# A two-layer graph kernel: three subtractions go to GpSimd, x's second half is loaded sooner, the bias split comes later

## The chip, the core and the metric

The kernel runs on one core of a Trainium2 chip. The metric is the device time of one execution in microseconds (us). The core has five engines, each with its own instruction queue: TensorE (PE, matrix products, with its weight load PEld), VectorE (DVE), ScalarE (ACT), GpSimd (POOL) and SyncE (SP, which here only starts transfers). They order their work by semaphores alone.

## What is computed

Two message-passing layers over a graph of 3125 nodes with 53125 edges. A message is a linear function of the target's row, the source's row and one number of the edge; messages are added up at their target, and self loops are added.

```python
def _mp_layer(x, src, dst, edge_attr, W, b):
    loops = jnp.arange(n); src2 = cat(src, loops); dst2 = cat(dst, loops)
    ea2 = cat(edge_attr, zeros)
    msg = jnp.concatenate([x[dst2], x[src2], ea2], axis=1) @ W + b
    return jax.nn.relu(jax.ops.segment_sum(msg, dst2, num_segments=n))
h = relu(_mp_layer(x, ..., W1, b1))          # 64 -> 128 columns
out = log_softmax(_mp_layer(h, ..., W2, b2)) # 128 -> 64 columns
result = layernorm(x + out)
```

## The kernel before

The sum over edges is made as a product with the adjacency matrix. That matrix (3125 x 3125, bf16) is built on the chip: edges are sorted by target, so every 5 targets own a window of at most 128 edges; there are 625 windows, handled in 79 sets of 8.

**Start.** DVE and PE find where each window's edges begin (`pick_row`, `offset`, the last step of `offset` raises `off_ready`, one count for each of 5 blocks j of 125 windows). GpSimd fetches each block's edges with an indirect transfer (`gather_edges(j)`, L400, into `pairs`, counted by `pairs_in[j]`) and the edges' numbers with another (`gather_attrs(j)`, L404). DVE turns block 0 into keys (L535 to L547), PE transposes them, ACT copies them to `keys` (`copy_keys`, L880, L882).

**The loop over sets.** For set k, DVE makes the one-hot matrices (`onehots(k)`, L569: one instruction over 8 windows, from set 12 on over 7, the eighth being made by GpSimd's `last_onehot(k)`, L441). PE multiplies them (`build(k)`, L1057, 8 products into one of two PSUM buffers) and ACT copies the result into the adjacency matrix (`evacuate(k)`, L909). `onehots(k)` waits until `build(k-3)` is done, since there are three one-hot buffers; `build(k)` waits for `evacuate(k-2)`. PE runs `build` 4 sets ahead of layer 1: in round b it builds set b + 4 and multiplies the 8 adjacency blocks of set b with x (`layer1`, L1079). Layer 1 of target group 0 waits for `evacuate(3)`. After its 12th product PE builds set 6 and only then goes on to the x of groups 12 to 24.

**x in three pieces.** x is float32, the products are bf16, so x is split into a high, a middle and a low piece in `x3`. ACT copies the high piece (`cast_x`, L864), a subtraction leaves a rest in `x_rest` (`rest_of_x`, L581), ACT copies the middle piece (`cast_middle_x`, L868), and another subtraction makes the low one (`low_of_x`, L586). This is done for groups 0 to 11 (i = 0, XA = 12) and 12 to 24 (i = 1). Layer 1 needs middle and low of the half it reads (`xm_ready`, `xl_ready`).

**Bias in three pieces.** The bias rows are split in the same way: `cast_bias(k)` (ACT, L860), `bias_rest(k)` (DVE, L593). When all three pieces are there (`bp_ready` 3), SP sends them with nine small transfers to `bw` (L1253); they are first used by `hidden(0)` near 56 us.

**Edge numbers.** DVE sums them (`attr_sums`, L556, one instruction a set, sets 16 to 20 for block 0). SP writes the sums to DRAM (L1258) and reads them back in another layout (L1261); GpSimd splits them (`split_sums(0)`, before its one-hot of set 24). SP's queue has the nine bias transfers ahead of L1258.

**SP's queue** at the start: targets (L1229), x's first half (L1231), three weight transfers, six bias transfers, a wait for `pairs_in[0]`, x's second half (L1244), two more bias rows.

All queues are written out by hand in this order; no planner reorders them.

Of the kernel before, what the change touches and what calls it, by code (L numbers as in the profile page):

```python
# [100 lines left out]
def gnn(nc, x, x_tiles, dst, edges, edge_attr, W1, b1, W2, b2, out, E):  # L101
# [3 lines left out]
    with ExitStack() as ctx:  # L105
# [260 lines left out]
        def _(gp):  # L366
# [31 lines left out]
            def gather_edges(j):  # L398
                gp.wait_ge(off_ready, j + 1)
                gp.indirect_dma_start(pairs[:, j, 0:2 * (SLOTS - LOOPS)], None, edges,  # L400
                                      bass.IndirectOffsetOnAxis(off_idx[:, j:j + 1], 0)).then_inc(pairs_in[j], 16)

            def gather_attrs(j):
                gp.indirect_dma_start(attrs[:, j, 0:SLOTS - LOOPS], None, edge_attr,  # L404
                                      bass.IndirectOffsetOnAxis(off_idx[:, j:j + 1], 0)).then_inc(attrs_in[j], 16)

            gather_edges(0)
            gather_attrs(0)
            gather_edges(1)
            gather_attrs(1)  # L410
            for j in range(2, J):
                gather_edges(j)
            for j in range(2, J):
                gather_attrs(j)
# [68 lines left out]
        def _(dve):  # L483
# [98 lines left out]

            def low_of_x(i, a, b):

                dve.wait_ge(xm_ready, i + 1)
                dve.tensor_tensor(x3[:, a:b, 2 * XC:2 * XC + C], x_rest[:, a:b, :], x3[:, a:b, XC:XC + C], ALU.subtract)\  # L586
                   .then_inc(xl_ready, 1)

            def bias_rest(k):

                before = brows[VHALF:128, :] if k == 0 else brest[VHALF:128, k - 1, :]
                dve.wait_ge(bp_ready, k + 1)
                dve.tensor_tensor(brest[VHALF:128, k, :], before, bpart[VHALF:128, k, :], ALU.subtract).then_inc(br_ready, 1)  # L593
# [41 lines left out]
            rest_of_x(0, 0, XA)  # L635
            bias_rest(0)
            dve.wait_ge(consts, 7)
# [6 lines left out]
            onehots(3)  # L644
            low_of_x(0, 0, XA)
            onehots(4)
            rest_of_x(1, XA, G)

            for k in range(5, NSETS):
# [3 lines left out]
                onehots(k)  # L653
                if k == 6:
                    low_of_x(1, XA, G)
                if k == 9:
                    bias_rest(1)
# [184 lines left out]
        def _(act):  # L842
# [26 lines left out]

            cast_bias(0)  # L870
            cast_x(0, 0, XA)
# [66 lines left out]
            def cast_middle(i):  # L938
                a, b = EPILOGUES[i]
                act.wait_ge(rest_ready, i + 1)  # L940
                act.activation(z3[:, a:b, C:2 * C], u[i % 2][:, 0:b - a, 0:C], ACT.Copy).then_inc(mid_ready, 1)

            evacuate(0)
            evacuate(1)
            cast_x(1, XA, G)
            for k in range(2, LEAD):
                evacuate(k)
            for b in range(NSETS):
                if b + LEAD < NSETS:
                    evacuate(b + LEAD)  # L950
                if b == 0:
                    cast_middle_x(1, XA, G)
                if b == 2:
                    cast_bias(1)
                if b == 6:
                    cast_bias(2)
# [271 lines left out]
        def _(sp):  # L1228
            sp.dma_start(dst_rows, dst).then_inc(dst_in, 16)  # L1229
            sp.wait_ge(dst_in, 16)  # L1230
            sp.dma_start(x_nat[:, 0:XA, :], x_tiles[:, 0:XA, :]).then_inc(xnat_in[0], 16)  # L1231
            sp.dma_start(w1c[:, :], W1[0:2 * C, :]).then_inc(w_in, 16)
            sp.dma_start(w2c[:, 0:C], W2[HID:2 * HID, :]).then_inc(w_in, 16)
# [5 lines left out]
            for m in range(1, EP):  # L1239
                at_m = VFROM + m * KB  # L1240
                sp.dma_start(brows[at_m:at_m + 3, :], row_b1.broadcast_to([3, HID])).then_inc(b_in, 16)
                sp.dma_start(brows[at_m + 3:at_m + KB, :], row_w1.broadcast_to([KB - 3, HID])).then_inc(b_in, 16)
            sp.wait_ge(pairs_in[0], 16)
            sp.dma_start(x_nat[:, XA:G, :], x_tiles[:, XA:G, :]).then_inc(xnat_in[1], 16)  # L1244
            sp.dma_start(b2w2[:, 0, :], b2.rearrange("(a n) -> a n", a=1).broadcast_to([Q, C])).then_inc(b2_in, 16)
# [69 lines left out]
```

## Time and profile before

| what | us |
|---|---|
| median of 3 runs | 195.45 (195.19 to 196.38) |
| the profiled execution, its time | 196.11 |
| the profiled execution, its span | 194.0 |
| PE busy in it | 173.6 |
| DVE busy in it | 161.8 |
| ACT busy in it | 114.5 |
| POOL busy in it | 99.2 |

The span runs from the first to the last instruction of one profiled execution. A row of a timeline gives the start, the duration, the engine, the line and the tiles written and read; what stands in square brackets is the idle time ahead of it and what ended that. Instructions overlap slightly at their ends, so the distance between starts is the real cost of one in a row of them. The chain of work that ended last is followed back from the last instruction.

### The profile page before, as it was taken

The page shows a single profiled execution, that of the slowest core. Times are in us where ns is not written, and L with a number is a line of the kernel's source. Part 1 is how long each engine was busy: PE and PEld are TensorE (multiplying, and loading weights), DVE is VectorE, ACT ScalarE, POOL GpSimd, SP SyncE. Part 2 cuts the span into 40 slices and gives each one's busy share as a digit, 9 for nine tenths or more (in the row PEclk, how much of TensorE's full clock was granted, in tenths as well). Part 3 has the DMA queues.
Part 4 walks back from the last instruction along what each step waited for, and adds up shares of the span by engine and source line. Part 5 has one row for each costly group of instructions (what it writes and reads, how often), then busy time and mean ns, then how long its engine had stood idle before and what let it go on. Part 6 is the DMA issues. An engine that isn't in the chain of part 4 may idle for free.

```text
span 194.0 us, 5193 instructions
## 1 busy us (share of the span) xinstructions
PE 173.6 (89%) x2050; PEld 157.6 (81%) x2051; DVE 161.8 (83%) x407; ACT 114.5 (59%) x197; POOL 99.2 (51%) x192
## 2 busy tenths in 40 slices
PE   7677577999699999989999999999999999999940
PEld 2124476998699898979999999999999999999940
DVE  0889999999997999999888979737619969889773
ACT  2425897888698989878989989972311102022201
POOL 6388504797697989699999969700000000000000
PEclk9969999999999999999999999999999999999996
DMA  1336200000000000000000000000000010100010
GB/s 44 103 89 155 57 3 2 6 1 4 1 6 1 4 1 4 2 1 4 0 3 0 5 3 0 0 3 5 0 0 5 8 35 0 42 9 22 20 25 20
DMA packets 9032, 3.35 MB, mean 17 GB/s; under 512 B 8240, under 2 KB 8557, under 8 KB 9007
## 3 DMA queue, kind: packets, MB, share of 16 engines
q1 hardware_dynamic: 8207, 2.08, 5.1%
q0 software_dynamic: 800, 0.93, 2.2%
q8 instruction: 17, 0.28, 0.6%
q14 instruction: 8, 0.07, 0.1%
HBM read 2.18 MB, written 0.81 MB: 15 GB/s over the span
## 4 chain that ended last, share of the span: by engine, by line
PE 59%; DVE 26%; DMA 7%; issue 3%; POOL 2%; ACT 0%; DVEq 0%; POOLq 0%
PE pset L1126 18%; DVE oh L569 15%; PE acc L1079 15%; PE acc L1126 9%; PE pset L1057 8%; DMA se<-se_scratch 3%; DMA adj<-in_edges,adj 3%; PE acc L1027 2%; PE epb L1120 2%; PE epb L1109 2%; DVE adj L556 2%; DMA se_scratch<-adj 2%; POOL oh L441 1%; PE epb L1097 1%; DVE adj L581 1%
## 5 line engine op out<-in xcount | busy, mean ns | idle before, releaser
L909 ACT ACTIVATE adj<-pset 125x1000 bf16<-125x1000 f32 (+1 forms) x79 | 78.5, 996 | 11.7 <-PE pset L1057 8.8
L441 POOL TENSOR_SCALAR oh<-iota,keys 128x125 bf16<-128x125 bf16 x132 | 78.3, 618 | 11.8 <-PE pset L1057 11.3
L569 DVE TENSOR_TENSOR oh<-iota_bank,keys 128x1764 bf16<-128x1764 bf16 (+4 forms) x81 | 83.1, 1052 | 0.5 <-PE pset L1057 0.4
L1079 PE MATMUL acc<-x,adj 125*125 125x195 bf16 x625 | 65.3, 248 | 0.3 <-DVE x L586 0.3
L1057 PE MATMUL pset<-oh 128*128 128x125 bf16 x625 | 48.2, 218 | 8.5 <-DVE oh L569 4.5
L1079 PEld LDWEIGHTS acc<-x,adj 125*125 125x125 bf16 x625 | 54.7, 137 | 0.9 <-issue 0.5
L1057 PEld LDWEIGHTS pset<-oh 128*128 128x128 bf16 x625 | 38.9, 97 | 12.7 <-ACT adj L909 6.0
L1126 PE MATMUL pset<-z,adj 125*125 125x192 bf16 x425 | 36.8, 246 | 0.0
L1126 PEld LDWEIGHTS pset<-z,adj 125*125 125x125 bf16 x425 | 35.5, 136 | 0.1
L988 ACT ACTIVATE x<-x 125x192 f32<-125x192 f32 (+2 forms) x6 | 2.6, 427 | 32.4 <-DVE x L737 32.4
L1126 PE MATMUL acc<-z,adj 125*125 125x192 bf16 x200 | 17.5, 246 | 0.0
L1126 PEld LDWEIGHTS acc<-z,adj 125*125 125x125 bf16 x200 | 16.8, 136 | 0.0
L601 DVE TENSOR_REDUCE u<-acc 125x65 f32<-125x195 f32 x25 | 8.9, 355 | 8.6 <-PE acc L1079 8.3
L1027 PE MATMUL acc<-adj 128*128 128x512 bf16 x31 | 11.3, 526 | 1.2 <-DVE adj L492 1.2
L1027 PEld LDWEIGHTS acc<-adj 128*128 128x128 bf16 x32 | 4.0, 127 | 6.5 <-issue 4.4
L400 POOL DMA_INDIRECT adj<-in_edges,adj x5 | 6.3, 1270 | 4.7 <-DVE adj L519 3.5
L728 DVE TENSOR_REDUCE x<-pset 125x64 f32<-125x192 f32 x17 | 5.4, 351 | 3.5 <-PE pset L1126 3.5
L556 DVE SCALAR_TENSOR_TENSOR adj<-adj 125x128 bf16<-125x128 f32 x25 | 7.4, 297 | 0.0
L404 POOL DMA_INDIRECT adj<-in_edge_attr,adj x5 | 6.0, 1208 | 1.5 <-issue 1.5
L1109 PE MATMUL epb<-turn,w1c 128*128 128x375 f32 x16 | 6.8, 504 | 0.0
L1120 PE MATMUL epb<-w2c,turn 128*125 128x128 f32 x48 | 6.8, 277 | 0.0
L622 DVE TENSOR_TENSOR u<-epb,z 125x192 f32<-125x192 f32 (+1 forms) x9 | 3.0, 337 | 4.1 <-ACT z L936 4.1
(125 smaller groups left out, 151.2 us busy)
## 6 DMA issues: line engine op xcount, KB each, us to landing
x_nat<-in_x_tiles SPq DMA_DIRECT2D x1, 406.2 KB
x_nat<-in_x_tiles SPq DMA_DIRECT2D x1, 375.0 KB
out<-x SPq DMA_DIRECT2D x2, 187.5 KB
out<-x SPq DMA_DIRECT2D x3, 93.8 KB
adj<-in_dst SPq DMA_DIRECT2D x1, 208.5 KB
bw<-adj SPq DMA_DIRECT2D x9, 1.0 KB
out<-x SPq DMA_DIRECT2D x1, 125.0 KB
adj<-in_edges,adj POOLq DMA_INDIRECT x5, 5.1
```

What stands on the lines that cost most here:

```text
L400: gp.indirect_dma_start(pairs[:, j, 0:2 * (SLOTS - LOOPS)], None, edges, bass.IndirectOffsetOnAxis(off_idx[:, j:j + 1], 0)).then_inc(pairs ...
L441: ins = gp.tensor_scalar(oh[k % 3][:, OWN, side, 0:Q], iota1[:, 0:Q], keys[:, place(k * SET + OWN), side, 0:1], None, ALU.is_equal)
L556: dve.scalar_tensor_tensor(out=se_junk[:, j * WD + r, :], in0=d_f[:, j, :], scalar=float(r), in1=attrs[:, j, :], op0=ALU.is_equal, op1=ALU ...
L569: ins = dve.tensor_tensor(out=oh[k % 3][:, at_w:at_w + m, :, 0:2 * PAIRS].rearrange("p w t (q e) -> p (w t) q e", e=2), in0=iota_p.unsquee ...
L601: dve.tensor_reduce(u[i % 2][:, m, C:2 * C + 1], acc[g % 2][0:Q, 0:XW].rearrange("p (t c) -> p c t", t=3), AX.X, ALU.add)\
L909: ins = act.activation(bands[c][0:Q, :, at_w:at_w + n * WD].rearrange("p h (w e) -> p h w e", e=WD), rows[:, 0:n, 0:WD * G].rearrange("p w ...
L1027: pe.matmul(acc[1][:, :], still[:, 0:128], still, start=True, stop=True)
L1057: ins = pe.matmul(pset[k % 2][:, i // 4, i % 4 * 128:i % 4 * 128 + WD * G], oh[k % 3][:, i, 0, :], oh[k % 3][:, i, 1, 0:Q], start=True, st ...
L1079: ins = pe.matmul(acc[g % 2][0:Q, 0:XW], block_of_adj(g, h), x3[:, h, 0:XW], start=(h == 0), stop=(h == G - 1))
L1109: pe.matmul(epb[:, 0, 0:n], w1c[:, :], flat(i)[:, 0:n], start=True, stop=False)
L1120: ins = pe.matmul(z_cols(b - a)[:, m, :], flat(i)[:, m * Q:(m + 1) * Q], w2c[:, :], start=True, stop=True)
L1126: ins = pe.matmul(bank2(g)[0:Q, :], block_of_adj(g, h), z3[:, h, :], start=(h == 0), stop=(h == G - 1))
```

## The change

Three of the four subtractions of x move from DVE to GpSimd: `low_of_x(0)`, `rest_of_x(1)` and `low_of_x(1)`; `rest_of_x(0)` stays on DVE. On GpSimd they stand behind the fourth gather of edges, with the fifth between the second and third of them, and four gathers of edge numbers come behind all that. ACT's `cast_x(1)` moves ahead of `evacuate(0)`, and `cast_middle_x(1)` from behind `evacuate(4)` to behind `evacuate(1)`. SP issues x's second half right behind the first, after a wait for the fourth offset in place of the first block's edges; weights and biases follow. The bias split moves back: `cast_bias(0)` from before `cast_x(0)` to round 2, `cast_bias(1)` from round 2 to 6, `cast_bias(2)` from 6 to 10, `bias_rest(0)` from before set 0 to behind set 8, `bias_rest(1)` from behind set 9 to behind set 12.

```diff
@@ gpsimd
+            def rest_of_x(i, a, b):
+                gp.wait_ge(xs_ready, i + 1)
+                gp.tensor_tensor(x_rest[:, a:b, :], x_nat[:, a:b, :], x3[:, a:b, 0:C], ALU.subtract).then_inc(xs_rest, 1)
+            def low_of_x(i, a, b):
+                gp.wait_ge(xm_ready, i + 1)
+                gp.tensor_tensor(x3[:, a:b, 2 * XC:2 * XC + C], x_rest[:, a:b, :], x3[:, a:b, XC:XC + C], ALU.subtract)\
+                  .then_inc(xl_ready, 1)
             gather_edges(0)
+            gather_edges(1)
             gather_attrs(0)
-            gather_edges(1)
-            gather_attrs(1)
-            for j in range(2, J):
-                gather_edges(j)
-            for j in range(2, J):
+            gather_edges(2)
+            gather_edges(3)
+            low_of_x(0, 0, XA)
+            rest_of_x(1, XA, G)
+            gather_edges(4)
+            low_of_x(1, XA, G)
+            for j in range(1, J):
                 gather_attrs(j)
@@ vector
             rest_of_x(0, 0, XA)
-            bias_rest(0)
...
             onehots(3)
-            low_of_x(0, 0, XA)
             onehots(4)
-            rest_of_x(1, XA, G)
...
                 onehots(k)
-                if k == 6:
-                    low_of_x(1, XA, G)
-                if k == 9:
+                if k == 8:
+                    bias_rest(0)
+                if k == 12:
                     bias_rest(1)
@@ scalar
-            cast_bias(0)
             cast_x(0, 0, XA)
...
+            cast_x(1, XA, G)
             evacuate(0)
             evacuate(1)
-            cast_x(1, XA, G)
+            cast_middle_x(1, XA, G)
...
-                if b == 0:
-                    cast_middle_x(1, XA, G)
                 if b == 2:
+                    cast_bias(0)
+                if b == 6:
                     cast_bias(1)
-                if b == 6:
+                if b == 10:
                     cast_bias(2)
@@ sync
             sp.dma_start(x_nat[:, 0:XA, :], x_tiles[:, 0:XA, :]).then_inc(xnat_in[0], 16)
+            sp.wait_ge(off_ready, 4)
+            sp.dma_start(x_nat[:, XA:G, :], x_tiles[:, XA:G, :]).then_inc(xnat_in[1], 16)
             sp.dma_start(w1c[:, :], W1[0:2 * C, :]).then_inc(w_in, 16)
...
-            sp.wait_ge(pairs_in[0], 16)
-            sp.dma_start(x_nat[:, XA:G, :], x_tiles[:, XA:G, :]).then_inc(xnat_in[1], 16)
```

## Rows read from the trace of the kernel before

**Rows 1.** Busy time of each engine in three stretches, with the granted clock (PEclk).
```profile
20.00:25.00 5.00, 2.55 (x34) 1.94 (x32) 5.00 (x6) 4.29 (x6) 2.41 (x2) 1.00 0.19 48
...
40.00:50.00 10.00, 9.10 (x122) 8.16 (x120) 9.93 (x23) 8.02 (x10) 7.27 (x14) 1.00 0.05 2
...
100.00:150.00 50.00, 50.00 (x632) 48.60 (x629) 35.83 (x66) 31.72 (x56) 23.27 (x40) 1.00 0.01 2
```

**Rows 2.** The chain that ended last, 7 to 47 us: start, us, what.
```profile
7.58 5.02 DMA adj<-in_edges,adj
...
16.06 4.55 DVE oh L569 x4
20.61 0.86 DVE x L586
...
22.59 0.93 DVE adj L581
...
25.76 0.93 DVE x L586
...
45.26 1.51 DMA se_scratch<-adj
```

**Rows 3.** Timeline of DVE, 11 to 45 us.
```profile
11.05 0.16 DVE L519 SCALAR_TENSOR_TENSOR adj<-adj 125x1 int32<-125x1 f16 x1
...
12.62 0.29 DVE L535 TENSOR_SCALAR adj<-adj,thr_neg 125x128 f32<-125x128 int32 x1 [0.64 <-DMA adj<-in_edges,adj]
...
15.40 0.36 DVE L593 TENSOR_TENSOR adj<-adj 64x128 f32<-64x128 f32 x1
15.80 0.23 DVE L638 COPY iota_bank<-iota 128x63 f32<-128x63 f32 x1
...
44.95 0.28 DVE L556 SCALAR_TENSOR_TENSOR adj<-adj 125x128 bf16<-125x128 f32 x1
```

**Rows 4.** The five edge gathers (L400): issue ns min/median/max, then time to landing.
```profile
L400 POOL DMA_INDIRECT adj<-in_edges,adj x5: 1212/1212/1501, 7.6 to 17.0; - x5
...
DMA to landing us min/median/max: 4.2/5.1/6.5
```

**Rows 5.** DMA queue of SP: packets, MB and share, 9.4 to 12.5 us.
```profile
q1 hardware_dynamic: 214, 0.08, 9.5%
```

**Rows 6.** The same queue, 12.6 to 18 us.
```profile
q1 hardware_dynamic: 182, 0.43, 23.1%
```

**Rows 7.** Timeline of SP's issues: x's second half, then the nine bias transfers.
```profile
12.61 0.26 SPq L1244 DMA_DIRECT2D x_nat<-in_x_tiles  x1
...
34.27 5.64 SPq L1253 DMA_DIRECT2D bw<-adj  x9
```

**Rows 8.** POOL's groups by line and shape: busy us, mean ns of one.
```profile
L441 POOL TENSOR_SCALAR oh<-iota,keys 128x125 bf16<-128x125 bf16 x132 | 78.3, 618 | 11.8 <-PE pset L1057 11.3 <-ACT keys L882 0.5
...
L425 POOL TENSOR_TENSOR se_rest<-se,stats 125x5 f32<-125x5 f32 x5 | 1.1, 218 | 0.4
...
L382 POOL CAST ident<-ident 128x125 bf16<-128x125 f32 x1 | 0.3, 291 | 0.1
```

**Rows 9.** Timeline of ACT, 15 to 28 us.
```profile
15.56 0.86 ACT L868 ACTIVATE x<-adj 125x768 bf16<-125x768 f32 x1
...
19.99 0.89 ACT L864 ACTIVATE x<-x_nat 125x832 bf16<-125x832 f32 x1
20.78 1.89 ACT L909 ACTIVATE adj<-pset 125x1000 bf16<-125x1000 f32 x2
...
27.57 0.31 ACT L860 ACTIVATE adj<-adj 64x128 bf16<-64x128 f32 x1
```

**Rows 10.** Timeline of PE, 22 to 24 us.
```profile
22.74 0.60 PE L1057 MATMUL pset<-oh 128*128 128x125 bf16 x8 [1.38 <-ACT adj L909]
23.18 0.84 PE L1079 MATMUL acc<-x,adj 125*125 125x195 bf16 x8
```

**Rows 11.** Timeline of POOL, the first one-hot that it makes.
```profile
30.89 1.20 POOL L441 TENSOR_SCALAR oh<-iota,keys 128x125 bf16<-128x125 bf16 x2 [8.18 <-PE pset L1057]
```

More of the change, by code:

```diff
@@ L581, in rest_of_x @@
                 dve.tensor_tensor(x_rest[:, a:b, :], x_nat[:, a:b, :], x3[:, a:b, 0:C], ALU.subtract).then_inc(xs_rest, 1)
[L583 to L587, printed above, removed]
             def bias_rest(k):
```

## The prediction, as put on record

> **What bounds the kernel now.** I read the busy time by stretch first, then the chain that ended last, then the timelines of the engines at the start. From 100 to 150 us PE is busy for all 50 us; from 40 to 50 DVE is busy 9.93 of 10 and PE 9.10; from 20 to 25 DVE is busy 5.00 of 5 and PE only 2.55 [rows 1]. So PE sets the end, but what it can start on is handed to it late by DVE. The chain goes through DVE's one-hots, and between them through three of DVE's subtractions for x, 0.86, 0.93 and 0.93 us of it; at 45.26 it passes to the DRAM write of block 0's edge sums [rows 2]. That write follows the last of DVE's attribute sums, at 44.95 [rows 3], and GpSimd and PE wait for its return. Before 12.6 us the chain is the first gather of edges, 5.02 us from 7.58 [rows 2], for which DVE idles 0.64 us [rows 3]. So the whole kernel hangs on how early DVE reaches its work of 45.26. Everything behind that point waits on other instructions of the chain and on nothing with a clock of its own, so a lead there is a lead at the end. I count the lead there.
>
> **First gather: lead 0.5.** Today three weight and six bias transfers run beside it: SP's queue moved 0.08 MB in 214 packets from 9.4 to 12.5 us [rows 5]. After the change these come later, and x's second half is issued only at the fourth offset's end, 11.05 + 0.16 = 11.21 [rows 3]. The five gathers land 4.2 to 6.5 us after their issue begins; the first has the longest issue, 1.50 us against 1.21 [rows 4]. With the best transfer it would land at 7.58 + 4.2 + 0.29 = 12.07. DVE is free at 12.62 - 0.64 = 11.98, so the gain lies between 0 and 0.62. I take 0.5, since the neighbours that the best gather lacked are what is taken away here.
>
> **Before the first one-hot: lead 0.3, less 0.07.** `bias_rest(0)` goes from in front of the iota copy, 15.80 - 15.40 = 0.40 us [rows 3]; it comes back behind set 8. But the one-hots also wait for ACT's copy of the keys, which comes from PE's transposes and moves with the gather alone; from the chain's order, with the first one-hot at 16.06 [rows 2] and the copy done near 15.67 (the middle cast follows it at 15.56 with a small overlap, [rows 9]), 0.33 of it can be used and I lose 0.02 to 0.1 to the wait. The first one-hot starts at 16.06 - 0.5 - 0.3 = 15.25. As the bias subtraction returns later, this is no lead at 45.26; the loss of 0.07 is.
>
> **Three subtractions off DVE: lead 2.72.** 0.86 + 0.93 + 0.93 [rows 2]. This is the gain if DVE never waits in their place.
>
> **What they cost on GpSimd.** The trace has no wide subtraction there. GpSimd's subtraction of 5 columns takes 0.218 us and its cast of 125 columns 0.291 [rows 8]: (0.291 - 0.21)/120 = 0.7 ns a column over a fixed 0.21 or so, which for 768 and 832 columns is 0.73 and 0.77 us. The compare of 125 columns takes 0.618 [rows 8], so 3.4 ns a column: 2.8 and 3.0. I take the middle, 1.8 and 1.9: two operands are read for each column where the cast reads one, while the compare does more per column than a subtraction.
>
> The Trainium skill (GPSIMD Engine Reference, "Performance versus the Vector engine") gives 4497 ns for a float32 `tensor_tensor` of 2048 columns. By that my estimate would be 1.69 and 1.83 us, the middle cast would come some 0.2 us sooner than below and the sum would be 2.5 in place of 2.3; no row of this trace has such an instruction, so it stays beside the sum.
>
> **Does anything wait for them?** I walk through the new order.
> - x's second half is issued at 11.25. Today it is issued at 12.61 [rows 7], and by 18.0 its queue had moved 0.43 [rows 6] of the 0.47 MB of x and the two bias rows behind it: about 5.4 us. It lands at 16.65. ACT's `cast_x(1)`, 0.89 us [rows 9], ends at 17.5. The first `evacuate` started at 18.05 today and would be due at about 17.0, so it is held 0.5; nobody needs it before `build(2)`.
> - `cast_middle_x(0)`, 15.56 + 0.86 today [rows 9], ends at 15.92. GpSimd's fifth edge gather, its seventh transfer, starts at 17.0 today, and each takes 1.21 and a gap of 0.3 [rows 4]; in the new order the fifth transfer is the fourth gather of edges and ends near 15.15. So `low_of_x(0)` runs 16.0 to 17.8 and `rest_of_x(1)` 17.8 to 19.7.
> - ACT ends `evacuate(1)` at 19.4, waits until 19.7, casts until 20.6 and then evacuates at 0.95 each (1.89 for two, [rows 9]): set 2 until 21.55, set 3 until 22.5.
> - PE: `build(4)` at 21.6 (22.74 today). The first eight products of layer 1 at 22.55 (23.18 today [rows 10]), `build(5)` until 23.8, four products, `build(6)` until 24.6. `low_of_x(1)`, after the fifth gather, ends at 23.15 and is hidden by 1.4 us.
> - ACT, always busy now: sets 4, 5, 6 until 25.75, `cast_bias(0)`, 0.31 [rows 9], until 26.05. DVE has nine one-hots of 1.115 (4.55 for four in a row with overlap, [rows 2], less 0.09) and comes to `bias_rest(0)` at 15.25 + 10.03 = 25.28. So **DVE waits 0.8 us there**: the queue of one-hots stands behind a bias subtraction that nobody needs soon. This is the new stall.
> - After that DVE is the slowest again. PE and ACT get 0.3 further ahead, as `bias_rest(1)` moves behind set 12.
> - The nine bias transfers occupy SP for 5.64 us, from 34.27 today [rows 7]. `cast_bias(2)` in round 10 comes at about 37.0, so SP is free at 42.65, and the sums' write is due at 45.26 - 2.35 = 42.9. Hidden with 0.25 us to spare; I charge 0.05.
> - The four gathers of edge numbers now end at 23.15 + 6.1 = 29.3. GpSimd's first one-hot began at 30.89 [rows 11] and is needed by `build(12)`, by my walk near 32.7. Hidden.
> - ACT's earlier bias casts, gone from the start, held nothing: `cast_x(0)` behind it was done before DVE needed it.
>
> **Sum.** 0.5 + 2.72 - 0.07 - 0.8 - 0.05 = 2.3 us. The profiled execution's span goes from 194.0 to 191.7 and its time from 196.11 to 193.8; against the median of 195.45, which lies 0.66 under it, the forecast is 193.2 us, 1.2% less.
>
> **Rivals.**
> - *A, the forecast*: gain 1.4 to 3.1. The upper end is a GpSimd as fast as its cast (middle cast right behind `evacuate(1)`, 0.3 us sooner, and the bias wait shrinks) with the wait of 0.8 nearly gone: 0.6 + 2.72 - 0.2. The lower end is no lead from the gather and a bias wait of 1.2. Chance 0.6.
> - *B, GpSimd at the compare's price*: 2.8 and 3.0 us. The pair in front of `cast_middle_x(1)` takes 2.1 us longer, ACT waits with all its evacuations behind the cast, layer 1 begins 2.1 later and DVE waits 2.9 at `bias_rest(0)` and before it for free one-hot buffers. Gain 0.2: 195.2 us. For it: it is the only arithmetic of GpSimd with many instances in the trace. Against: a compare with a scalar of each partition is another form. Chance 0.2.
> - *C, the load or SP's queue eats it*: x's second half lands 1 us later because four gathers cross it, and the same chain through ACT moves by 0.9; or the nine bias transfers end behind the sums. Gain 1.0: 194.4. Chance 0.12.
> - *D, slower*: GpSimd takes the compare's 0.618 us for 125 columns in full proportion, 4.9 ns a column, that is 3.8 and 4.1. The pair takes 4.2 us longer than I assume, `low_of_x(1)` then ends behind `build(6)` by a further 0.8, and DVE loses more than the 2.72 it saved: 2.3 - 4.2 - 0.8 = 2.7 us lost, 198.1. It decides from a pair price of about 6 us (no gain) and 8 us (1% slower). PE would also idle 3 us in a row; today's granted clock stays 1.00 with PE busy 2.55 of 5 [rows 1], which leaves open what a longer gap does. Chance 0.08.
>
> **How the numbers follow.** The likeliest is A, 193.2 us. The range reaches from A's best, 192.3, over C and B, to 195.6, leaving out D and a little at each end. A measurement of this kernel tells about 1% (1.95 us) from no change. A's gain lies above that in three quarters of its cases, the rest with B and C is within 1%: faster 0.47, same 0.45, slower 0.08.
>
> **What would show it.** In the changed trace: DVE starts L535 near 12.1; the first one-hot near 15.25; GpSimd's subtractions take 1.8 to 1.9 us each; ACT's middle cast of x's second half starts near 19.7; layer 1 starts near 22.5; DVE idles about 0.8 us ahead of `bias_rest(0)`, released by ACT; SP's write of the first edge sums is issued near 42.9 and not behind the bias transfers; from there every row stands 2.3 us earlier. I am wrong if a subtraction takes over 2.5 us, if the first gather still lands at 12.6, or if SP's write waits for SP itself.

## The result, and the profile after

Over 14 executions each the changed kernel took 194.53 us in the middle (193.82 to 196.10), the kernel before 195.76 (195.17 to 196.38). The ratio is 0.995, with a 95% interval of 0.993 to 0.9971: faster by 0.5%, or 1.0 us (the two middles are 1.2 us apart), where 1.2% had been forecast. A second group of 12 executions gave the same ratio, 0.995 (0.9925 to 0.9975). The time lies inside the range given. Two executions at a much lower clock throughout (298.94 us of the kernel before, 199.47 us of an edited kernel) are left out of every ratio and middle.

The profiled execution of the changed kernel does not show that: its span is 192.0 us against 194.0, with a time of 194.07 against 196.11, a gain of 2.0. Its start goes almost as the prediction walked it. (The changed kernel has line numbers of its own: its one-hots are L583, its bias transfers L1258, its write of the sums L1263.) DVE's timeline, with the lines that answer to [rows 3]:

```profile
11.93 0.29 DVE L549 TENSOR_SCALAR adj<-adj,thr_neg 125x128 f32<-125x128 int32 x1
12.13 0.56 DVE L550 TENSOR_SCALAR adj<-adj 125x128 f32<-125x128 int32 x1
...
15.09 10.12 DVE L583 TENSOR_TENSOR oh<-iota_bank,keys 128x2016 bf16<-128x2016 bf16 x9 [0.27 <-ACT keys L886]
25.96 0.29 DVE L601 TENSOR_TENSOR adj<-adj 64x128 f32<-64x128 f32 x1 [0.75 <-ACT adj L865]
...
42.61 0.28 DVE L570 SCALAR_TENSOR_TENSOR adj<-adj 125x128 bf16<-125x128 f32 x1
```

The keys begin at 11.93 without any wait (forecast 12.1), nine one-hots run without a break, and then DVE waits 0.75 us for ScalarE's bias cast (forecast 0.8). POOL's timeline:

```profile
11.45 1.21 POOL L404 DMA_INDIRECT adj<-in_edge_attr,adj  x1 [0.30 <-issue]
...
15.82 1.54 POOL L415 TENSOR_TENSOR x<-adj,x 125x768 bf16<-125x768 f32 x1
17.80 1.76 POOL L410 TENSOR_TENSOR adj<-x_nat,x 125x832 f32<-125x832 f32 x1 [0.44 <-ACT x L869]
...
20.99 1.67 POOL L415 TENSOR_TENSOR x<-adj,x 125x832 bf16<-125x832 f32 x1
```

The three subtractions take 1.54, 1.76 and 1.67 us. ACT's timeline, which answers to [rows 9]:

```profile
16.83 0.90 ACT L869 ACTIVATE x<-x_nat 125x832 bf16<-125x832 f32 x1 [1.09 <-DMA x_nat<-in_x_tiles]
17.63 1.88 ACT L913 ACTIVATE adj<-pset 125x1000 bf16<-125x1000 f32 x2
19.60 0.91 ACT L873 ACTIVATE x<-adj 125x832 bf16<-125x832 f32 x1
20.41 2.77 ACT L913 ACTIVATE adj<-pset 125x1000 bf16<-125x1000 f32 x3
```

ACT now stands still for x's second half, in front of the first evacuation; before, it asked for it at 19.99 and had no wait [rows 9]. PE's timeline ([rows 10]):

```profile
21.44 0.61 PE L1062 MATMUL pset<-oh 128*128 128x125 bf16 x8 [1.05 <-ACT adj L913]
22.33 0.89 PE L1084 MATMUL acc<-x,adj 125*125 125x195 bf16 x8 [0.28 <-ACT adj L913]
```

And SP's issues ([rows 7]):

```profile
37.25 5.64 SPq L1258 DMA_DIRECT2D bw<-adj  x9
42.94 0.46 SPq L1263 DMA_DIRECT2D se_scratch<-adj  x1
44.80 0.27 SPq L1266 DMA_DIRECT2D se<-se_scratch  x1
```

The write of the edge sums is issued at 42.94, 2.3 us sooner than the 45.26 of [rows 2], and right behind the ninth bias transfer. The chain shows that it takes longer from there:

```profile
42.94 1.85 DMA se_scratch<-adj
44.80 2.92 DMA se<-se_scratch
```

1.85 us where it was 1.51 [rows 2]. So of the lead of 2.3 us 2.0 are left, down to the end.

The same chain shows what the start now hangs on:

```profile
11.19 5.61 DMA x_nat<-in_x_tiles
...
16.83 0.91 ACT x L869
...
17.80 1.77 POOL adj L410
...
19.60 0.91 ACT x L873
20.51 1.78 ACT adj L913 x2
...
25.62 0.32 ACT adj L865
...
25.96 0.29 DVE adj L601
```

It no longer passes through the first gather, the first keys or DVE's first one-hots. It goes from the fourth offset over the landing of x's second half to ACT, and comes back to DVE only at the bias subtraction, for which DVE had been waiting.

The two profiled executions are 2.04 us apart (196.11 and 194.07), the middles only 1.23. The one of before lies 0.35 over the middle of its 14, the one of the changed kernel 0.46 under that of its own: 2.04 - 0.35 - 0.46 = 1.23. What is to be explained is why that pair of traces is not the typical pair.

### The profile page after: what moved, and what is told of

It is laid out like the page before. It is cut to its first block, busy times and chain, and to the rows that moved or that the text cites. A ratio compares the mean times of both kernels' runs of the same rounds, so it can differ in the third digit from the quotient of the medians.

```text
span 192.0 us, 5193 instructions
## 1 busy us (share of the span) xinstructions
PE 173.6 (90%) x2050; PEld 157.6 (82%) x2051; DVE 159.1 (83%) x404; ACT 113.7 (59%) x197; POOL 104.3 (54%) x195
## 4 chain that ended last, share of the span: by engine, by line
PE 60%; DVE 19%; DMA 8%; issue 4%; POOL 3%; ACT 3%; DVEq 0%; POOLq 0%
PE pset L1131 18%; PE acc L1084 15%; DVE oh L583 10%; PE pset L1062 9%; PE acc L1131 9%; DMA se<-se_scratch 3%; DMA x_nat<-in_x_tiles 3%; PE acc L1032 2%; PE epb L1125 2%; PE epb L1114 2%; DVE adj L570 2%; ACT adj L913 2%; DMA se_scratch<-adj 2%; POOL oh L455 1%; DVE adj L531 1%
## 5 line engine op out<-in xcount | busy, mean ns | idle before, releaser
L583 DVE TENSOR_TENSOR oh<-iota_bank,keys 128x1764 bf16<-128x1764 bf16 (+4 forms) x81 | 83.0, 1053 | 0.8 <-PE pset L1062 0.4
L913 ACT ACTIVATE adj<-pset 125x1000 bf16<-125x1000 f32 (+1 forms) x79 | 77.7, 994 | 9.6 <-PE pset L1062 7.4
L1131 PE MATMUL acc<-z,adj 125*125 125x192 bf16 x200 | 17.5, 246 | 0.0
L1131 PEld LDWEIGHTS acc<-z,adj 125*125 125x125 bf16 x200 | 16.8, 137 | 0.0
L400 POOL DMA_INDIRECT adj<-in_edges,adj x5 | 6.4, 1285 | 5.1 <-DVE adj L533 4.4
L939 ACT ACTIVATE base<-epb 125x192 f32<-125x192 f32 (+1 forms) x9 | 2.9, 318 | 6.1 <-PE epb L1125 6.1
```

The lines of the kernel that those rows point to most:

```text
L583: ins = dve.tensor_tensor(out=oh[k % 3][:, at_w:at_w + m, :, 0:2 * PAIRS].rearrange("p w t (q e) -> p (w t) q e", e=2), in0=iota_p.unsquee ...
L913: ins = act.activation(bands[c][0:Q, :, at_w:at_w + n * WD].rearrange("p h (w e) -> p h w e", e=WD), rows[:, 0:n, 0:WD * G].rearrange("p w ...
L1131: ins = pe.matmul(bank2(g)[0:Q, :], block_of_adj(g, h), z3[:, h, :], start=(h == 0), stop=(h == G - 1))
```

## The experiments

All of them are edits of the changed kernel unless said otherwise. Ratios are to the kernel before, run in the same group; for the changed kernel itself the ratio is 0.995 in both groups in which it ran. It did not run in the groups of `before_again`, `fill`, `bias_mix` and `dve_subs`, nor in that of `port_free`, `cold`, `combo` and `port_combo` (on another chip than the second group); these are compared with it through the ratios.

### The changed kernel again

> The changed kernel once more, nothing edited: what the other kernels of this group are compared with, and a second trace of it. Theory 1 (the walk was right, the forecast was read off an execution of the kernel before that lay 0.35 us over its own median): the lead at SP's write of the first edge sums is 2.3 us again and the middle of the runs is 1.2 to 2.0 us under the kernel before. Theory 2 (a part of the executions of the changed kernel has one more delay of about 1.5 us, which the profiled one did not have): the runs fall again in two groups, near 194.2 and near 195.8.

Ratio 0.995 (0.9925 to 0.9975). Both theories have a part. Sorted by mean granted clock, its 12 executions fall in two groups: eight with a clock over 0.975 took 193.42 to 194.18, four at 0.975 or less took 194.97 to 195.46. With the first 14 executions: 18 of 26 are over 0.975 and 8 at or under it. The middles of the groups differ by 1.3 us (193.96 and 195.31) and 1.5 us (194.33 and 195.80). For the kernel before in the same group they differ by 0.4 (15 executions with 195.29, 8 with 195.69). The bound of 0.975 was set after the times were known, and it is a rough mark: one execution of 195.20 had a clock of 0.994. The lead at the write of the sums was not 2.3 again: it is issued at 43.36, where the first changed trace has 42.94, as x's second half, on which the chain runs here too, came later (ACT's cast at 17.33 instead of 16.83) and DVE's wait grew to 1.05 us. First ACT's timeline of this trace, then DVE's:

```profile
17.33 0.90 ACT L869 ACTIVATE x<-x_nat 125x832 bf16<-125x832 f32 x1 [1.42 <-DMA x_nat<-in_x_tiles]
```

```profile
26.47 0.29 DVE L601 TENSOR_TENSOR adj<-adj 64x128 f32<-64x128 f32 x1 [1.05 <-ACT adj L865]
```

Its chain at the write:

```profile
43.36 1.81 DMA se_scratch<-adj
```

### The kernel before again

> The kernel before, nothing edited, for a second trace of it. The profiled execution of before had a span of 194.0 us, while half of its 23 executions of the first group lie under 193.4. If the execution on which the prediction rests was a late one, this trace shows where: the same order of work with a span nearer 193.3, and some 0.6 us less at one place, most likely in a transfer (the first gather, or the edge sums' way through DRAM), and the lead of the changed kernel over it is then under 2 us from there on. If the span is again 194.0, that reason falls.

One execution of 195.61 us, span 193.6. The trace on which the prediction rests was a late one: the write of the sums is issued at 44.66 here and at 45.26 there. The place is at the start, DVE's instructions for the first keys. This trace first, then the rows next to [rows 3] in the earlier one:

```profile
12.45 0.29 DVE L535 TENSOR_SCALAR adj<-adj,thr_neg 125x128 f32<-125x128 int32 x1 [0.41 <-DMA adj<-in_edges,adj]
...
12.90 0.23 DVE L540 TENSOR_SCALAR adj<-adj 125x128 f32<-125x128 f32 x1
...
15.47 4.55 DVE L569 TENSOR_TENSOR oh<-iota_bank,keys 128x2016 bf16<-128x2016 bf16 x4
```

```profile
13.08 0.57 DVE L540 TENSOR_SCALAR adj<-adj 125x128 f32<-125x128 f32 x1
```

L540 took 0.23 us here and 0.57 there; the first gather was 0.17 sooner. At the write, SP's timeline of this trace has:

```profile
44.66 0.27 SPq L1258 DMA_DIRECT2D se_scratch<-adj  x1
46.15 0.28 SPq L1261 DMA_DIRECT2D se<-se_scratch  x1
```

The two traces put beside the two of the changed kernel, in us:

| trace | first keys | held instruction | first one-hot | DVE's bias wait | write of sums | span |
|---|---|---|---|---|---|---|
| before | 12.62 | L540 0.57 | 16.06 | none | 45.26 | 194.0 |
| before again | 12.45 | none (0.23) | 15.47 | none | 44.66 | 193.6 |
| changed | 11.93 | L550 0.56 | 15.09 | 0.75 | 42.94 | 192.0 |
| changed again | 12.07 | L550 0.58 | 15.27 | 1.05 | 43.36 | 192.1 |

Against this second trace of before the lead at the first one-hot is 0.2 to 0.4 us, not 0.8; at the write it is 1.3 to 1.7, and at the end 1.5 to 1.6. These are two traces of each kernel; how often L540 is held in the kernel before is not known.

### GpSimd's transfers kept away from the keys

```diff
             gather_edges(0)
             gather_edges(1)
-            gather_attrs(0)
+            gp.wait_ge(key_ready, 1)
             gather_edges(2)
-            gather_edges(3)
             low_of_x(0, 0, XA)
             rest_of_x(1, XA, G)
-            gather_edges(4)
+            gather_edges(3)
             low_of_x(1, XA, G)
+            gather_edges(4)
```

(and all five gathers of edge numbers behind it)

> The changed kernel with GpSimd waiting for the first keys ahead of its third transfer, and with the order edges 2, subtraction, subtraction, edges 3, subtraction, edges 4, all edge numbers. In every trace of a changed kernel VectorE's tile instruction at L550 takes 0.52 to 0.63 us instead of 0.22 and ends with GpSimd's third transfer (12.66 us in the first trace); in the trace of before the next instruction at L540 took 0.57 and ended with a transfer, in the second trace of before it took 0.23. If a transfer's issue on GpSimd blocks these instructions, L550 takes 0.22 us here and the first one-hot starts 0.3 us sooner, at 14.8; the subtractions start no later than now. If the long L550 has another cause it stays at 0.5. The whole gains 0 to 0.3 us, since ScalarE's wait for x's second half comes behind it.

```profile
11.90 0.29 DVE L549 TENSOR_SCALAR adj<-adj,thr_neg 125x128 f32<-125x128 int32 x1
12.11 0.22 DVE L550 TENSOR_SCALAR adj<-adj 125x128 f32<-125x128 int32 x1
...
15.26 10.12 DVE L583 TENSOR_TENSOR oh<-iota_bank,keys 128x2016 bf16<-128x2016 bf16 x9 [0.80 <-ACT keys L886]
```

L550 takes 0.22 us, as expected: what held it was the transfer that GpSimd was issuing. In the changed kernel that issue runs from 11.45 to 12.66, L550 begins 0.68 us into it and ends at 12.69. Over all traces, ten such `tensor_scalar` instructions began 0.60 to 0.72 us into an issue; they took 0.52 to 0.63 us instead of 0.22 to 0.29, and each ended 0.02 to 0.03 us behind it. One that begins earlier is not held: in the second trace of before L540 began 0.43 us into an issue, and in the kernel `x_at_once` (below) L550 began 0.27 us into one and took 0.22, which is the exception to what the expectation says of every trace. A `scalar_tensor_tensor` that began 0.70 us into one took its usual 0.29. The Trainium skill (SBUF — State Buffer, "Who interferes with whom") says that VectorE's `tensor_scalar` can enter a mode with two ports, that it then shares a port pair with GpSimd, and that whoever has it first keeps it for its instruction. The traces agree on the blocking; they differ in that only the later part of an issue blocks. That it is the port pair which blocks here was not tested by itself.

The first one-hot was not sooner here (15.26), since it waits 0.80 us for ACT's copy of the keys: in this execution the granted clock was 0.5 from 7.4 to 14.2 us and TensorE's transposes of the keys came late. In the last experiment, where the clock was full again from 11.2 us, the same edit brought the first one-hot to 14.59. The later one-hots cost nothing either: they begin 0.17 us later than in the changed kernel's first trace, VectorE's wait ahead of the bias subtraction shrinks from 0.75 to 0.47 us, and the write of the sums is issued at 42.94 in both. The chain of this trace runs over x's second half and ACT, past the keys. The ratio is 0.9936 (0.991 to 0.9962), which does not differ from 0.995 beyond the intervals. The mean clock of the 11 executions also shows how rough a mark it is: eight are at 0.975 or less, and one of these, the profiled one at 0.973, is the fastest of all with 193.88; its low stretch lies at the start only.

### The clock: idle products taken away, and added

```diff
             for k in range(LEAD):
                 build(k)
-                if k < LEAD - 1:
-                    keep_going(1)
```

> The changed kernel without the three idle products between the first four builds, so that TensorE is idle for more of 17 to 22 us. If a low stretch of the clock behind that idle time costs the changed kernel 1.0 to 1.5 us in a part of its executions, more than half of them show it here: middle at 194.9 to 195.6, and the low ones have the lower mean clock. If the clock there does not matter, the middle stays within 0.3 us of the changed kernel's 194.2 to 194.5.

The ratio is 0.9989 (0.997 to 1.0008), middle 195.95 (the kernel before had 196.06 on this chip), all 12 executions at a mean clock of 0.974 or less: the whole gain is gone. Put beside the changed kernel's executions of the higher clock, which lie 0.7% under the kernel before, the delay is some 1.2 us, near the 1.3 to 1.5 us between its two groups above. PE's timeline in the trace, which is one of the faster executions (195.04):

```profile
21.33 1.02 PE L1062 MATMUL pset<-oh 128*128 128x125 bf16 x8 [1.00 <-ACT adj L913]
22.22 1.57 PE L1084 MATMUL acc<-x,adj 125*125 125x195 bf16 x8
23.58 1.05 PE L1062 MATMUL pset<-oh 128*128 128x125 bf16 x8
```

A build takes 1.02 to 1.05 us instead of 0.60, eight products of layer 1 take 1.57 instead of 0.89. The busy time of 21 to 25 us, first in this kernel, then in the changed one (columns as in [rows 1]):

```profile
21.00:25.00 4.00, 3.67 (x30) 3.53 (x31) 3.38 (x4) 2.51 (x4) 3.51 (x3) 0.57 0.19 41
```

```profile
21.00:25.00 4.00, 3.28 (x45) 3.11 (x46) 4.00 (x4) 3.48 (x5) 3.51 (x3) 1.00 0.18 40
```

PE is busier and gets 30 instead of 45 products done, at a granted clock of 0.57 (1.2 GHz for most of the time) instead of 1.00 (2.4 GHz). In the four microseconds before this PE had been busy for 1.81 of 4.00 us in this kernel and 2.30 in the changed one. These slowed products stand in the chain of this trace, in front of ACT's bias cast; the write of the sums is issued at 43.90.

The opposite edit puts work into the gap ahead of the build of set 4:

```diff
             for b in range(NSETS):
+                if b == 0:
+                    keep_going(4)
```

> The changed kernel with four idle products on TensorE ahead of the build of set 4, where it stands idle for 1.05 to 1.27 us at 20.3 us. In the trace of the kernel with the later bias subtraction the granted clock was 0.50 from 22.56 to 25.97 us, right behind this gap; builds took 1.04 instead of 0.60 us there. In the first group the changed kernel's executions with a mean clock of 0.975 or less were those of 194.97 to 195.46 us. If the low stretch behind this gap is the second group, it goes away: no execution over 194.7, middle 0.2 to 0.4 us lower. If the low clock there has another cause or costs nothing, a third of the executions stays at 195 or more.

Ratio 0.992 (0.9893 to 0.9947), six executions from 193.40 to 194.76. One is above the bound named (194.76, at a clock of 0.970), so the edit does not remove the low stretch in every execution. The ratio goes the expected way, but the intervals overlap.

A third edit fills an earlier gap, between the second and the third row product:

```diff
             for j in range(J):
+                if j == 2:
+                    keep_going(5)
                 pe.wait_ge(pick_ready, j + 1)
```

> The changed kernel with five more idle products on TensorE in its gap at 6.6 to 7.8 us, ahead of the third row product. The granted clock fell to 0.50 at 9.8 us after this gap and stayed there for 3.4 us. If the delay of some executions is that this low stretch falls on the key transposes or the first builds, the low stretch at the start goes away and the runs form one group near 194. If the clock has nothing to do with it, the two groups stay and the middle does not move by more than 0.2 us.

Ratio 0.9924 (0.9899 to 0.9948). The six executions have a clock of 0.981 to 0.987, and five lie in 193.72 to 194.30. The sixth, 194.88, is the profiled one, at 0.986 and without a low stretch before 187 us, where PE has no work left. So low clock is not the only thing that makes one late. x's second half came late there (cast at 17.54), but that explains only a part: the write is issued at 43.62, 0.3 us later than in the second changed trace, while the span is 1.0 us longer. The rest arises behind the write and stays open. Nor does this edit show anything of the stretch that it aims at, since the second changed trace has no low stretch at the start either.

Taken together, 1 of 22 executions of the four kernels with added idle products has a mean clock of 0.975 or less, against 8 of 26 of the changed kernel and 12 of 12 of the one with products taken away.

### The bias split

```diff
-                if k == 8:
+                if k == 10:
                     bias_rest(0)
```

> The changed kernel with the first bias subtraction of VectorE behind set 10 instead of set 8. The trace has VectorE idle for 0.75 us ahead of it, released by ScalarE. If that wait is the new stall on the path, as the prediction had it, the span shortens by 0.5 to 0.75 us, unless SP's nine bias transfers, which end at 42.9 us, then hold up the write of the edge sums: in that case the gain is about 0 and the write starts right behind them again at 42.9.

Ratio 0.9952 (0.9929 to 0.9974): no gain. The expectation had named SP's transfers for that case. The write of the sums does stand directly behind them, at 44.30 after 38.61 + 5.64 us, but VectorE's last sum ends at 44.25 too, so the trace does not show that SP held it. In the two traces of the changed kernel both also end at the same time, within 0.01 us. This trace has a low stretch of the clock from 22.6 us as well, so its absolute times say little. The next edit moves SP's transfers as well:

```diff
-                if k == 8:
+                if k == 9:
                     bias_rest(0)
-                if k == 12:
+                if k == 11:
                     bias_rest(1)
@@ scalar
-                if b == 6:
+                if b == 4:
                     cast_bias(1)
-                if b == 10:
+                if b == 8:
                     cast_bias(2)
```

> The changed kernel with the bias split tightened: first bias subtraction behind set 9, second behind set 11, second and third cast in rounds 4 and 8. The nine bias transfers of SP then begin near 35 us instead of 37.3 and end near 41, ahead of the edge sums at 42. If both the wait of 0.75 us ahead of the first bias subtraction and SP's nine transfers in front of the edge sums are on the path, the write of the sums starts 0.6 to 0.8 us earlier, lands in 1.5 instead of 1.85 us, and the fast executions are 0.9 to 1.1 us shorter than the changed kernel. If only the transfer queue counts, 0.3. If neither, 0.

Ratio 0.990 (0.987 to 0.993). SP's part of its trace:

```profile
35.65 5.64 SPq L1258 DMA_DIRECT2D bw<-adj  x9
43.59 0.27 SPq L1263 DMA_DIRECT2D se_scratch<-adj  x1
45.09 0.27 SPq L1266 DMA_DIRECT2D se<-se_scratch  x1
```

With SP free since 41.3 the way from the write's issue to the read's is 1.50 us again instead of 1.86. That holds over all traces: where the write follows the nine transfers directly it takes 1.68 to 1.93 us (nine traces), where SP had been free 1.48 to 1.51 (five traces). The execution has a low stretch of the clock from 22.7 to 26.1 (builds of 1.04 us), hence the late 43.59, and still took 194.13; the middle is 193.94. The gain of 0.5% over the changed kernel, with intervals that overlap a little, fits 0.9 us, though it cannot be split into the wait and the queue.

### Undoing parts

The three subtractions back on VectorE, behind sets 3, 3 and 5, all else as changed:

```diff
             onehots(3)
+            low_of_x(0, 0, XA)
+            rest_of_x(1, XA, G)
             onehots(4)
...
                 onehots(k)
+                if k == 5:
+                    low_of_x(1, XA, G)
```

> The changed kernel with the three subtractions of x back on VectorE (behind sets 3, 3 and 5), all else as changed: loads, bias, and ScalarE's order. The prediction counts 2.72 us for taking them off VectorE, less the 0.75 us that it then waits for the bias. If that is right this kernel is 1.5 to 2.2 us slower than the changed one in fast executions, so about as fast as the kernel before or 0.3 us slower. If the gain comes from the loads and not from the subtractions, it is within 0.5 us of the changed kernel.

Ratio 1.0079 (1.0054 to 1.0103), so 1.3% or 2.5 us slower than the changed kernel, a little more than expected. The subtractions themselves cost what they did (0.95, 1.01 and 1.01 us). The rest I put down to ScalarE's new order, which puts the middle cast ahead of the evacuations: in this trace it waits for VectorE's subtraction until 21.29, PE's build of set 4 starts at 23.14 after 1.91 us of idle time, and the clock is low from 24.4 to 27.8. How much of the 2.5 us each of these is was not separated. What the run does show is that the gain needs the subtractions on GpSimd: without them the other changes leave the kernel 0.8% slower than the one before.

SP's wait for the fourth offset taken away:

```diff
-            sp.wait_ge(off_ready, 4)
             sp.dma_start(x_nat[:, XA:G, :], x_tiles[:, XA:G, :]).then_inc(xnat_in[1], 16)
```

> The changed kernel with SP's wait for the fourth offset taken away, so that x's second half is issued at 4.9 us and is there long before ScalarE asks for it. If the delay of some executions comes from x's second half landing late (ScalarE waits for it in front of the first evacuation), these runs form one group, without those near 195.8, and ScalarE's wait of 1.1 us ahead of the second cast is gone. The first gather now has this transfer beside it and may land up to 0.6 us later, as in the kernel before: then the fast group is 0 to 0.6 us slower than the changed kernel. If the delay has another cause, there are still two groups.

Ratio 1.0095 (1.006 to 1.013), 1.45% or 2.8 us slower than the changed kernel. The expectation missed by far. ACT's wait for x is gone (cast at 17.97, with no idle time), but the first gather takes 7.00 us instead of 4.4, and here the chain does pass through it:

```profile
7.61 7.00 DMA adj<-in_edges,adj
14.63 0.29 DVE adj L549
```

The write of the sums is issued at 45.57, 2.6 us later than in the first changed trace: what the gather lost is found again there one for one. The edit lets the weights and biases go out earlier too, but they alone cost little: beside them, without x's second half, the gather took 5.02 and 4.79 us in the two traces of before. The place of x's second half is thus a balance: earlier it delays the keys, later it delays ScalarE. The five executions (196.17 to 197.90) are too few to say whether the two groups are gone.

### Together

The tighter bias split and the four idle products:

```diff
+                if b == 0:
+                    keep_going(4)
...
-                if k == 8:
+                if k == 9:
                     bias_rest(0)
```

(with the other lines of the bias edit above)

> The changed kernel with the tighter bias split (first two subtractions behind sets 9 and 11, later casts in rounds 4 and 8) and with four idle products ahead of the build of set 4. If the bias wait and SP's nine transfers are worth 0.6 to 1.1 us and the low clock stretch behind the gap costs its executions another 1.0, this has a middle of 193.2 to 193.6 and no execution over 194.2. If the two only hide behind each other it stays at 193.9.

Ratio 0.9883 (0.9858 to 0.9908), six executions from 193.42 to 194.15, all at a clock of 0.982 or more. The middle of 193.71 lies above the range named, on a chip where the kernel before took 196.06 instead of 195.4; none is over 194.2. With GpSimd's transfers moved as well:

> All three edits that should help together: GpSimd's transfers out of the way of the keys, the tighter bias split, and the idle products ahead of the build of set 4. If they act at different places, 0.2 to 0.3 us less than with the last two alone, so 193.0 to 193.4. If x's second half is the next bound, the same as with the two.

Ratio 0.9856 (0.9826 to 0.9887), middle 193.08 of four executions (192.66 to 193.40), where 0.2 to 0.3 us under the last kernel had been expected and 0.6 came. It has the lowest ratio of all, 3.0 us below the kernel before and by the ratios 0.9% below the changed one; that it beats the last kernel is not shown, as the intervals overlap. DVE in its trace:

```profile
11.98 0.22 DVE L550 TENSOR_SCALAR adj<-adj 125x128 f32<-125x128 int32 x1
...
14.59 11.40 DVE L583 TENSOR_TENSOR oh<-iota_bank,keys 128x2016 bf16<-128x2016 bf16 x10 [0.27 <-ACT keys L886]
26.03 0.29 DVE L601 TENSOR_TENSOR adj<-adj 64x128 f32<-64x128 f32 x1
```

The first one-hot is 0.5 us sooner than in the changed kernel, and the bias subtraction no longer waits. ACT's cast at 16.80 still waits 1.56 us for x's second half, and the chain goes over its landing and not over the keys, so that landing is the bound at the start.

## Why the prediction was right and wrong

**What bounds the kernel, and the count at 45.26: right.** In each pair of a trace of before and one of the changed kernel the lead at the write of the sums is the lead at the end within 0.3 us. In the first pair what is lost behind the write is lost in its own transfer.

**The base of the sum: the step that failed first.** Every lead was counted from one execution of the kernel before, in which L540 had been held for 0.34 us. The first one-hot was forecast for 15.25 and came at 15.09 and 15.27, right in absolute time. But against an execution of before that is not held the lead there is 0.2 to 0.4, not 0.8, and at the write 1.3 to 1.7. One execution was taken as the kernel. Its time of 196.11 stood in the prediction as 0.66 over the median, and 0.66 is more than a quarter of the gain forecast. Subtracting the whole gain from the median was not warranted unless the late part was common to both kernels, and it was not. Against the 14 executions of before the base was 0.35 too high.

**First gather, 0.5: right in itself, but no term of this sum.** The first keys begin 0.4 to 0.7 us sooner than in the two traces of before (11.93 and 12.07 against 12.45 and 12.62). GpSimd's third transfer now runs beside them, 0.55 us later than it stood before since GpSimd waits 0.91 us for the second offset, and holds L550 for 0.34 and 0.36 us. Neither the lead nor its loss reaches the end: DVE then waits 0.75 and 1.05 us for ACT, whose work hangs on x's second half. The prediction had this wait, but counted 0.5 and 0.8 as if each stood alone; a gather 0.5 us later would, by these rows, have shortened the wait by as much, and its sign of being wrong, a first gather that lands at 12.6, would not have moved the end. The kernel in which L550 is free bears this out: one-hots 0.17 us later, the wait shorter, the write at 42.94 again. The lead matters where the chain does pass through the keys, as in `x_at_once` and `dve_subs`.

**Three subtractions off DVE, 2.72, and the new wait, 0.8: right.** They are gone from DVE's timeline and the wait in front of the bias subtraction is 0.75 and 1.05 us; it ends at 25.96 and 26.47, where 26.05 had been forecast. Putting them back costs 2.5 us, in part for the orders of the other engines.

**The price on GpSimd, 1.8 and 1.9: right within 0.3.** Measured are 1.54, 1.76 and 1.67 us, 2.0 to 2.1 ns a column. By the Trainium skill (GPSIMD Engine Reference, "Performance versus the Vector engine") it would be, as an estimate from its figure for 2048 columns, 1.69 and 1.83; the trace agrees with it within 0.16 us: 1.54 against 1.69, 1.76 and 1.67 against 1.83. Rivals B and D fall on this number.

**SP's queue, 0.05: the term was mis-sized.** The write was issued at the time forecast (42.94 against 42.9), but behind nine transfers it took 1.85 and 1.81 us where it had taken 1.51 and 1.48, so 0.3 us more; 0.05 had been charged. The prediction asked only whether SP was free to issue, not what was still on its way in the same queue.

**x's second half at 16.65: nearly right, but as a fixed number.** It came at 16.8 to 17.5 in the two traces of the changed kernel and that of the third idle edit. It lies on the chain of both traces of the changed kernel, so each tenth moves ACT's cast, GpSimd's subtraction and DVE's bias subtraction: between the two traces ACT's cast moves by 0.50 us, the bias subtraction by 0.51 and the write by 0.42. The prediction let it hold only the first evacuation. In the kernel before ACT asked for x 2 us after that half had landed by the prediction's own estimate (18.0 and 19.99). Rival C had the place and a chance of 0.12.

**The clock: left open under rival D, put at nothing in the sum, and it was on the path.** The prediction took 1.00 for granted since the trace of before showed 1.00 there with PE half idle. Traces of variants show stretches at a granted clock of 0.5 between 21 and 28 us (22.7 to 26.1, 24.4 to 27.8), and in 8 of 26 executions of the changed kernel a mean clock of 0.975 or less goes with a time 1.3 to 1.5 us longer. In the kernel before the same difference in mean clock goes with 0.05 to 0.4 us in the three groups; a likely reason is that its PE waits for DVE there (0.77 us ahead of a build at 24.79) and has time to lose, but no trace of it has a low stretch in that place. So the change put PE on the path just where its clock is uncertain. The kernel without idle products, in which the whole gain is gone, and three traces of edited kernels whose chains go through slowed products (1.24 to 1.43 us for eight of layer 1) show the mechanism; that it is this stretch in each of the 8 executions is inferred from the mean clocks, since those were not traced. Where the bias subtraction comes later, the price is less: the executions at 0.975 or less are 0.5 us (later by two sets) and 0.6 us (the tighter split) slower in the middle than the others.

In sum: forecast 2.3. Against a typical execution of before 0.4 less, 0.3 less at SP, 0 to 0.5 less for x's landing, and in a third of the executions 1.4 less for the clock. With the middle of the term for x that leaves 1.3 to 1.4 us in the executions with the higher clock, where 1.33 was measured between the middles (193.96 and 195.29), and 0.9 over all, where 1.0 to 1.2 was measured.

What stays open: how much of bias wait and SP queue each is worth alone, how often the kernel before is held at L540, what delays an execution behind the write, and what sets the clock's low stretch in some executions and not in others.

## What to carry to other kernels

Before a gain of 1% is worked out of one trace, ask what in that trace is not in each execution; the distance between the profiled execution's time and the median is the first warning, and it must be explained before the whole gain is taken off the median. A change that removes the slack of an engine makes everything uncertain on that engine count: here a landing time that had cost nothing and a clock that had cost little began to cost 0.5 and 1.4 us. Where the new order makes an engine wait, a lead ahead of that wait is no lead; ask the chain behind the releaser instead. And work moved to another queue should be looked at for what stands behind it on its way, not only for whether the queue is free.

## What the runs showed of the hardware

An issue of an indirect transfer on GpSimd holds a VectorE `tensor_scalar` on 32-bit data: begun 0.60 to 0.72 us into the 1.21 us of the issue, it ended with it (0.52 to 0.63 us instead of 0.22 to 0.29); begun 0.27 or 0.43 us into one, it took 0.22 or 0.23. The first gather took 4.4 us with the weights, the biases and x's second half held back until the fourth offset, 4.8 and 5.0 with weights and biases beside it, and 7.00 with x's second half (406 KB) beside it as well. Nine transfers of 1 KB directly ahead in SP's queue lengthened the next one from 1.5 to between 1.7 and 1.9 us. GpSimd subtracts float32 columns at 2.0 to 2.1 ns each, and VectorE's one-hots beside it kept their 1.12 us.
